# Fused cross-attention and sign-weight FFN block: who issues the first eight loads

## The reference

```python
q = einsum('bsd,ed->bse', layernorm(x), wq)
k = concatenate([ctx, einsum('bsd,ed->bse', layernorm(x), wk)], axis=1)
v = concatenate([ctx, einsum('bsd,ed->bse', layernorm(x), wv)], axis=1)
attn = softmax(einsum('bqd,bkd->bqk', q, k) / sqrt(512))
x = x + tanh(g_xattn) * einsum('bqk,bkd,ed->bqe', attn, v, wo)
h = relu(einsum('bsd,hd->bsh', layernorm(x), sign(up_weight)) * up_scale)
x = x + tanh(g_ffn) * einsum('bsh,dh->bsd', h, sign(down_weight)) * down_scale * output_scale
```

## Time and profile before

| what | us |
| --- | --- |
| median of 3 runs | 601.21 |
| lowest and highest of them | 600.84, 603.96 |
| the profiled execution | 599.61 |
| its span, first to last instruction | 597.8 |
| busy in the span: PE, PEld, DVE, ACT, POOL | 587.9, 486.5, 380.9, 289.9, 118.8 |

### The profile page before, as it was taken

The page is one execution under the profiler, slowest core; times in us unless marked ns, Lnnn a source line. Parts: engine busy times, 40 slices in busy tenths (PEclk is TensorE's granted clock), DMA queues, the critical chain, the costliest instruction groups (busy, mean ns, idle before and its releaser), DMA issues.

```text
span 597.8 us, 7100 instructions
## 1 busy us (share of the span) xinstructions
PE 587.9 (98%) x2738; PEld 486.5 (81%) x2738; DVE 380.9 (64%) x532; ACT 289.9 (48%) x426; POOL 118.8 (20%) x111
## 2 busy tenths in 40 slices
PE   8999999899999999999999999999999999999997
PEld 6888888788888888888888888888887878888885
DVE  4697717788454587454587786755459734766654
ACT  3784401574321464321566565655659444645531
POOL 4006300403003002003011016232322002242002
PEclk9999999999999999999999999999999999999999
DMA  8614014032010153020112223120111301230011
GB/s 298 213 71 138 5 31 139 7 105 72 1 72 0 18 194 106 1 71 1 71 42 85 87 70 106 35 72 35 59 49 35 136 11 66 72 141 36 0 71 70
DMA packets 20097, 43.21 MB, mean 72 GB/s; under 512 B 4832, under 2 KB 4832, under 8 KB 19680
## 3 DMA queue, kind: packets, MB, share of 16 engines
q1 hardware_dynamic: 20064, 42.76, 20.9%
HBM read 36.45 MB, written 6.30 MB: 72 GB/s over the span
## 4 chain that ended last, share of the span: by engine, by line
PE 93%; DVE 3%; DMA 2%; ACT 1%; SPq 0%; issue 0%; ACTq 0%
PE proj L540 34%; PE score L670 19%; PE turn L655 12%; PE score L573 9%; PE score L540 5%; PE proj L655 5%; PE proj L573 4%; PE turn L532 2%; PE score L804 2%; DMA rows<-in_x 1%; DMA raw_ctx<-in_ctx_turned 1%; PE turn L638 1%; PE proj L638 1%; DVE four_x L1190 0%; DVE four_x L1323 0%; DVE turned_x L1318 0%
## 5 line engine op out<-in xcount | busy, mean ns | idle before, releaser
L670 PE MATMUL score<-down_signs,hid_split 128*128 128x512 f32 x512 | 133.8, 390 | 0.6 <-DVE normed L1552 0.5
L670 PEld LDWEIGHTS score<-down_signs,hid_split 128*128 128x128 f32 x512 | 95.8, 188 | 21.7 <-DVE hid_split L1519 0.9
L540 PE MATMUL proj<-probsT,four_x 128*128 128x512 f32 x384 | 89.3, 391 | 0.0
L540 PEld LDWEIGHTS proj<-probsT,four_x 128*128 128x128 f32 x384 | 71.5, 188 | 14.6
L540 PE MATMUL proj<-four_x,weights 128*128 128x512 f32 x336 | 77.2, 390 | 1.6 <-ACT raw_new L899 1.6
L540 PEld LDWEIGHTS proj<-four_x,weights 128*128 128x128 f32 x336 | 62.9, 188 | 15.1 <-ACT raw_new L899 2.0
L465 POOL TENSOR_TENSOR four_x<-raw_ctx,four_x 128x2048 fp32r<-128x2048 f32 x7 | 32.6, 4655 | 192.6 <-ACT four_x L885 192.6
L1519 DVE TENSOR_TENSOR hid_split<-hid,hid_split 128x512 fp32r<-128x512 f32 x64 | 44.0, 690 | 15.8 <-ACT hid_split L1109 15.6
L893 ACT ACTIVATE four_x<-proj 128x512 fp32r<-128x512 f32 x32 | 19.1, 597 | 67.6 <-PE proj L540 67.6
L540 PE MATMUL proj<-weights,four_x 128*128 128x512 f32 x192 | 51.9, 405 | 0.0
L655 PE MATMUL turn<-ops_b,up_ops 128*128 128x512 f32 x192 | 51.8, 391 | 0.0
(11 more groups left out here) (128 smaller groups left out, 871.3 us busy)
## 6 DMA issues: line engine op xcount, KB each, us to landing
raw_w<-in_ffn_w SPq DMA_DIRECT2D x24, 512.0 KB, 3.3
raw_ctx<-in_ctx_turned SPq DMA_DIRECT2D x4, 1024.0 KB, 5.3
raw_ctx<-in_ctx SPq DMA_DIRECT2D x4, 1024.0 KB, 5.8
result<-rows SPq DMA_DIRECT2D x16, 256.0 KB, 2.0
rows<-in_x SPq DMA_DIRECT2D x3, 1024.0 KB, 7.5
turned_x<-in_x_turned SPq DMA_DIRECT2D x3, 1024.0 KB, 5.3
rows_away<-rows SPq DMA_DIRECT2D x1, 2048.0 KB, 14.5
rows<-rows_away SPq DMA_DIRECT2D x1, 2048.0 KB, 7.8
```

Of the source, the lines that this page charges most:

```text
L540: last = pe.matmul(bank, lhs(l), rhs(r), start=start and i == 0, stop=stop and i == 2)
L670: last = pe.matmul(wide(r), hid_split[:, n % HR, s, r * P:(r + 1) * P], down_signs[:, chunk_of(q), :], start=(q == 0 and s == HI), stop=(q ...
```

## The change

The four loads of the key weights leave SyncE's list and become the first four instructions of ScalarE, ahead of its first activation. SyncE issues the four row tiles one behind another. No wait is added or taken away, and no destination, size or semaphore is another.

```diff
-            for half in ((0, 1), (2, 3)):
-                for r in half:
-                    sp.dma_start(rows[:, r, :], x_v[0, :, r, :]).then_inc(x0_in[r], 16)
-                for e in half:
-                    sp.dma_start(raw_of[W_K][:, e, :], wk[:, e].rearrange("p c n -> p (c n)")).then_inc(wk_in[e], 16)
+            for r in range(RT):
+                sp.dma_start(rows[:, r, :], x_v[0, :, r, :]).then_inc(x0_in[r], 16)
             sp.dma_start(raw_of[W_Q], wq.rearrange("p e c n -> p e (c n)")).then_inc(w_in[W_Q], 16)
...
+            for e in range(DC):
+                act.dma_start(raw_of[W_K][:, e, :], wk[:, e].rearrange("p c n -> p (c n)")).then_inc(wk_in[e], 16)
```

## The result

| | before | changed |
| --- | --- | --- |
| median of 9 runs each, us | 601.06 | 603.40 |
| lowest and highest | 599.94, 603.96 | 602.42, 605.49 |
| the profiled execution | 599.61 | 603.12 |
| its span | 597.8 | 601.3 |

The ratio to the kernel before is 1.0050, with a 95% interval of 1.0034 to 1.0066: 2 to 4 us slower. The forecast was 600.2, 0.9 under the median before, with a range up to 602.9. The sign was wrong, and the time lies 0.5 us beyond the range.

The account below looks back on a forecast made before the run. TensorE, busy 587.9 of 597.8 us, was taken as the bound, loads mattering only where it waits at the start. 599.61 - 1.0 = 598.6 for the profiled execution, set against the median 601.21: 600.2 us, range 599.0 to 602.9.

Parts of the forecast that it names:

- the 48: TensorE's 48 key matmuls after the 32; forecast to move from 17.71 to 16.7 us.
- The formula: Predicts when TensorE's 32 matmuls start from the landings of x1, x2 and wk1; 11.16 us before, 10.2 forecast.
- H: When high parts of turned tiles 0 and 1 are ready: max(X1 + 3.80, W1 + 1.62), forecast 9.1 us.
- S: Start of TensorE's 32 matmuls: max(H + 1.06, x2's landing + 2.37); 11.16 us before, forecast 10.2.
- X1: Landing of row tile x1: 4.0 us before, put at 5.3 for sharing with wk0.
- the slow stretch: Loads from 3.5 to 6.5 us: 178 GB/s, DMA engines busy 0.67; a second queue was to fill the hole.
- W1: Landing of key block wk1: 8.15 us before, forecast 7.1.
- The 1.0 us of gain: At the start: 3.0 us at 178 instead of 272 GB/s, 1.04 us, recovered if two queues fill the hole.
- rival 1: At the start loads: one engine pool, x2 and wk1 keep their places; no change, 601.2 us; chance 0.20.
- rival 2: At the start loads: x1 served third, lands at 6.75; loss 0.45 us, up to 1.85; chance 0.20.
- Rival 3: TensorE's start: late x1 causes a 2.5 to 2.8 us pause, clock falls, 40 matmuls lose 3.3 us; chance 0.04.
- rival 4: ScalarE's loads issue slowly, 1.1 us apiece or more, costing what exceeds 2.9 us; folded into rival 2, no own chance.

Follow-up runs that it names:

- first profile: The changed kernel, key loads moved from SyncE to ScalarE in the kernel before; its profiled execution took 603.12 us against 599.61.
- second profile: The changed kernel run once more without alteration, beside the kernel before on another chip: 603.48 us against 600.17, ratio 1.0050.

## Why the prediction was wrong

**The bound was read rightly.** The start of the 32 matmuls sets the 48, and these set the end. The formula holds: with x1 at 7.17 it gives H = 10.97 and S = 12.03, and with the 6.55 us from there to the 48 (17.71 - 11.16) they start at 18.6. The changed kernel with 47 matmuls on ones, which keeps its clock, measured 18.65.

**The step that failed is the value taken for X1, and behind it the reading of the slow stretch.** I took the 178 GB/s at a busy share of 0.67 as engines without work, which a second queue could give them. The runs show that the work itself was slow: at another pitch the same stretch carries 259 to 337 GB/s on one queue. So two queues did not fill the hole, they brought it forward to 1.5 to 3.5 us, onto x0 and x1. X1 was 7.0 against my 5.3; W1 was 7.55 against my 7.1, rightly earlier, and worth nothing because x1 now binds. The 1.0 us of gain was the price of a hole that more work would fill; measured, the late tile costs 0.76 to 0.94 us instead. The forecast treated the key blocks as bytes like others, although rival 1 already named "pieces 8 KB apart". Its weight there should have gone to rival 2: if the key blocks are slow by themselves and run beside x1, x1 is late.

**Rival 2 was the right mechanism.** X1 of 7.0 lies just beyond its 6.75, and the price of the late tile alone, 0.94 us, lies between its 0.45 and its bound of 1.85. It had 0.20.

**Rival 3 came true with it, at 0.04.** Its condition, a pause of 2.5 us or more, was a consequence of rival 2 and not a matter of chance beside it. With tile 1's statistics at 7.01 its rule (the turn 1.7 behind them) gives 8.7; measured 8.71. Its price of 3.3 us, all 40 matmuls slow, was too high: in the first profile the clock was back for the 40 and the turns and the matmuls on ones paid, 1.13 us. In the second profile, where the clock stayed low past 14 us, the same comparison gives 21.15 - 18.65 = 2.5 us. The 0.208 us that it used for a slow matmul stands in rows whose granted clock reads 1.00, so it was no reading of a low clock. Behind the longest pause of all, 6.53 us, the 40 took 6.70 us, against 5.06 with the clock kept.

**Rival 1 failed, and rival 4 did not occur.** An issue on ScalarE cost 0.48 us. The rule cited for rival 1, from the Trainium skill's page "DMA: Bandwidth & Descriptors", section "Issuing engines are not separate DMA queues", says that a second issuing engine saves only issue time. The runs agree in that no gain came; taken alone it would have made the change cost nothing, and here it costs 2 to 4 us, most of it by moving who shares with whom. By the Trainium skill's section "Queues, rings and completion order" of the same page, a DMA engine goes round between the queues with work. That fits x0 at 5.4 beside wk0 at 5.8 and x1 at 7.0 beside wk1 at 7.5: the landings now come in pairs.

**A second step failed at 91 us.** I said that this point moves along with TensorE. It also hangs on a store and a load of the facts, whose slack was 0.6 us in the profile before, and whose time varies by more than that. In the first profile it cost 1.35 us, in the second 0.28. Why the store took 12.0 us and not 10.6 stays open.

The sum as measured: 0.94 us for the late tile, 1.13 for the clock and 1.35 for the facts make 3.42 of the 3.5 us between the two spans. In the second profile the first two make 3.44 us, the clock 2.5 of them. The sum of the forecast had -1.0 for the first and nothing for the other two.

## What to carry to other kernels

When a transfer is slow while the DMA engines are partly idle, find out whether it lacks work or is slow by its own access pattern before giving it a second queue; a second queue makes the slow transfer a neighbour of the urgent one. Put the loads that the first engine in the chain waits for alone at the front, and price a late first tile together with the clock that a longer pause of TensorE costs. Where a layout in HBM is free to choose, try another pitch first: here it gave 0.2 to 0.3% (for 4 and 10 KB the interval reaches to no gain), and the queue gave none.

## What the runs showed of the hardware

- Loads of 128 pieces of 2 KB from HBM: with pieces 8 KB apart the stretch from 3.5 to 6.5 us carried 178 and 181 GB/s; with 4 and 10 KB it carried 337 and 297, and with the pieces one behind another 285, 317 and 259 in three profiles. All this is with one queue and the order of the kernel before, row tiles and key blocks mixed.
- A pause of TensorE of 1.09 to 1.53 us left the granted clock at 1.00 in four profiles; behind pauses of 2.83, 2.95 and 3.50 us stretches stood at 0.64, 0.51 and 0.50. Before the 72 matmuls near 107 us pauses of 1.37 to 2.01 us left it at 1.00 in thirteen profiles, and one of 1.95 us was followed by 0.72 in the fourteenth.
- A load of 256 KB in pieces 8 KB apart, issued on ScalarE's queue at 4.26, when SyncE's queue held three of 1 MB, took 7.3 us; issued first of all, beside x0, it had taken 5.1.
- A store of 4 KB of row facts took 10.6 to 12.0 us to land, more from chip to chip than between most kernels.
